# A four-layer pre-norm network on one core: seven of eight groups' first norm and top-8 routing moved from the projection block into the first expert stage

## The reference, cut to what matters

```python
x = x + _L0_attn_ref(_layernorm(x), ...)      # state-space scan, ends in a projection with Wout
x = x + _L0_ffn_ref(_layernorm(x), ...)       # top-8 of 64 experts plus a shared one
x = x + _L1_attn_ref(_layernorm(x), ...)
...
# _L0_ffn_ref
affinity = sigmoid(einsum('bsh,he->bse', hidden_states, router_w))
top_scores, top_idx = top_k(affinity, 8)
top_w = top_scores / (sum(top_scores) + 1e-09)
routed = sum over e of  router_mask[e] * (silu(x @ gate[e]) * (x @ up[e])) @ down[e]
```

## Time and profile before

| | us |
|---|---|
| median of 3 runs | 1939.16 |
| lowest and highest | 1934.07, 1939.63 |
| the profiled execution | 1942.1 |
| its span, from first to last instruction | 1940.4 |
| projection block, first instruction to the first expert instruction | 325.9 to 399.3 |
| first expert stage, 264 chunks | 399.3 to about 1110 |

### The profile page before, as it was taken

The page is one execution under the profiler, slowest core; times in us unless marked ns, Lnnn a source line. Parts: engine busy times, 40 slices in busy tenths (PEclk is TensorE's granted clock), DMA queues, the critical chain, the costliest instruction groups (busy, mean ns, idle before and its releaser), DMA issues.

```text
span 1940.4 us, 25449 instructions
## 1 busy us (share of the span) xinstructions
PE 1724.4 (89%) x8004; PEld 1318.3 (68%) x8004; DVE 1185.5 (61%) x2758; ACT 979.3 (50%) x1906; POOL 852.3 (44%) x866
## 2 busy tenths in 40 slices
PE   6989998779999899999999888889899888888799
PEld 6979997757767677776767655656665555555565
DVE  5542215767677777767686825444356666677765
ACT  3612001656556656565656667666545444445442
POOL 3841201335555545454545453444457666651100
PEclk9989558789999999999999989898899888889999
DMA  6001001087332323233223452221001101002233
GB/s 85 1 2 24 1 1 33 17 198 180 107 93 91 98 85 98 88 98 93 93 88 118 122 149 66 66 86 42 28 12 33 29 23 23 23 31 74 81 109 93
DMA packets 131183, 134.92 MB, mean 70 GB/s; under 512 B 56614, under 2 KB 75306, under 8 KB 131050
## 3 DMA queue, kind: packets, MB, share of 16 engines
q1 hardware_dynamic: 120904, 132.35, 24.5%
q10 hardware_dynamic: 10146, 0.94, 0.6%
HBM read 127.93 MB, written 5.31 MB: 69 GB/s over the span
## 4 chain that ended last, share of the span: by engine, by line
PE 39%; DVE 18%; ACT 12%; issue 7%; POOL 4%; DMA 2%; SPq 1%; DVEq 0%; ACTq 0%; POOLq 0%
PE ypsum L1156 7%; PE flow_G L100 4%; PE flow_G L102 3%; PE flow_G L101 3%; DVE flow_a L1701 2%; DVE flow_a L1707 2%; PE flow_U L100 2%; DVE flow_phi L1485 2%; PE flow_U L101 2%; PE flow_U L102 2%; POOL flow_alo L1790 2%; ACT flow_ahi L1186 1%; ACT xn_tokens L1218 1%; PE flow_side L100 1%; DVE flow_at_rneg L1673 1%
## 5 line engine op out<-in xcount | busy, mean ns | idle before, releaser
L1790 POOL TENSOR_TENSOR flow_alo<-flow_a,flow_ahi 128x512 fp32r<-128x512 f32 x264 | 341.6, 1294 | 339.8 <-ACT flow_ahi L1186 339.3
L100 PE MATMUL flow_G<-xn_hi,flow_hi 128*128 128x512 f32 x520 | 283.9, 546 | 37.6 <-DVE flow_a L1701 22.4
L1701 DVE TENSOR_TENSOR flow_a<-flow_G,flow_mask 128x512 f32<-128x512 f32 x256 | 175.7, 686 | 160.8 <-ACT flow_G L1360 135.4
L1360 ACT ACTIVATE flow_G<-flow_G 128x512 f32<-128x512 f32 x256 | 149.0, 582 | 141.1 <-PE flow_G L102 140.5
L101 PE MATMUL flow_G<-xn_lo,flow_hi 128*128 128x512 f32 x520 | 212.6, 409 | 0.0
L102 PE MATMUL flow_G<-xn_hi,flow_lo 128*128 128x512 f32 x520 | 212.1, 408 | 0.0
L1707 DVE TENSOR_TENSOR flow_a<-flow_U,flow_a 128x512 f32<-128x512 f32 x296 | 204.7, 691 | 9.9
L1186 ACT ACTIVATE flow_ahi<-flow_a 128x512 fp32r<-128x512 f32 x264 | 165.4, 627 | 86.6 <-DVE flow_a L1707 85.5
L1799 POOL TENSOR_TENSOR flow_b<-flow_b,flow_mask 128x512 f32<-128x512 f32 x96 | 126.8, 1327 | 148.5 <-ACT flow_b L1364 77.7
L1799 POOL TENSOR_TENSOR flow_a<-flow_a,flow_mask 128x512 f32<-128x512 f32 x96 | 127.8, 1342 | 105.8 <-ACT flow_a L1364 54.4
L100 PEld LDWEIGHTS flow_G<-xn_hi,flow_hi 128*128 128x128 f32 x520 | 102.2, 197 | 103.9 <-issue 42.2
(11 more groups left out here) (535 smaller groups left out, 3936.3 us busy)
## 6 DMA issues: line engine op xcount, KB each, us to landing
flow_mask<-mask_rows_top SPq DMA_DIRECT2D x512, 128.0 KB, 3.0
flow_mask<-mask_rows_top SPq DMA_DIRECT2D x64, 256.0 KB, 3.2
flow_mask<-mask_rows_zone SPq DMA_DIRECT2D x64, 256.0 KB, 3.2
flow_mask<-mask_rows_steps SPq DMA_DIRECT2D x32, 256.0 KB, 4.0
x<-in_L_attn_x SPq DMA_DIRECT2D x8, 256.0 KB, 5.9
flow_raw<-in_L_ffn_expert_gate_k SPq DMA_DIRECT2D x16, 128.0 KB, 3.6
flow_raw<-in_L_ffn_expert_up_k SPq DMA_DIRECT2D x16, 128.0 KB, 3.6
flow_raw<-in_L_ffn_expert_down_k SPq DMA_DIRECT2D x16, 128.0 KB, 3.9
```

The source lines that it names most:

```text
L100: pe.matmul(out, w_hi, x_hi, start=start, stop=False)
L1360: act.activation(gate, gate, ACT.Silu).then_inc(ev["r_done"], 1)
L1701: dve.tensor_tensor(out, G[at % 2].psum[:, :], weight, ALU.mult).then_inc(ev["t_done"], 1)
L1790: pool.tensor_tensor(alo[i][:, :], acts[i][:, :], ahi[i][:, :].bitcast(F32), ALU.subtract)\
```

## The change

The projection block keeps the product with `wout` and the addition to `x` for all eight groups, but norm, router and top-8 choice for group 0 only, written out in line. The other seven groups get a new kind of side step, "pro", in the flow block: `stats`, `moments`, `rstd`, `normalize`, `x_turn`, `hi`, `lo`, `affinities`, `choose_0` to `choose`, `weights`, `rows`. Group 1's lie in group 0's chunks, group 2's from chunk 29 to 50, group g's (g from 3) in frame g - 2. `exponents` goes to the front of ACT's part of the projection block (its two parameters are loaded first, under a semaphore of their own), the low parts of the 14 matrices go from POOL to DVE, some mask tables of POOL's behind the first norm, and the slabs and the one remaining weight row lie in SBUF where the split experts come later. So `rows_gone` is dropped: DVE waits for the slabs before the low part of chunk 3, and for group 0's row before that of chunk 20.

```diff
-ROUTE_LINKS = {1: 8, 2: 3, 3: 21}
+ROUTE_LINKS = {0: 5, 1: 8, 2: 3, 3: 21}
+LATER_OVER, ROWS_OVER = 3, 20
...
     def place(self, kind, l, g, off):
+        if kind == "pro":
+            if g == 1:
+                return off - (4 if off < 10 else 16)
+            if g == 2:
+                return self.hosts[0].chunks + (off - 5 if off < 10 else off - 21 if off < 28 else off - 20 if off < 31 else off - 19)
+            return (g - 2) * self.hosts[0].chunks + off
...
+PRO_STEPS = {"pe": ((7, "x_turn"), (26.5, "affinities"), (33.7, "weights")),
+             "act": ((4.7, "normalize"), (8, "hi"), (27.5, "affinities"), (34.7, "weights")),
+             "dve": ((1, "stats"), (1.5, "moments"), (9, "lo"), (28, "choose_0"), (29, "choose_1"), (30, "choose_2"), (31, "choose")),
+             "pool": ((2.5, "rstd"),), "sp": ((35.7, "rows"),)}
...
-        def rows_gone(eng):
-            for g in range(GROUPS):
-                eng.wait_ge(k.mask_out[g], 16)
-            eng.wait_ge(k.later_out, 32)
...
-                    if h.index and c == 0:
-                        pe.wait_ge(ev["lo"], plan.norm["att", h.index, g] + 1)
+                    if c == 0 and (h.index or g):
+                        pe.wait_ge(ev["lo"], plan.norm["att" if h.index else "pro", h.index, g] + 1)
...
                 def split_first(c):
+                    if c == LATER_OVER:
+                        dve.wait_ge(k.later_out, 32)
+                    if c == ROWS_OVER:
+                        dve.wait_ge(k.mask_out[0], 16)
...
+                def choose_top8(g, part):
...
+                    if part == 0:
+                        dve.wait_ge(ev["aff"], n + 1)
+                        for j in range(GT):
+                            last = dve.max(best[:, j, :], aff64[:, j, :])
...
+                    if part == 1:
+                        for j in range(GT):
+                            dve.match_replace(marked64[:, j, :], best[:, j, :], aff64[:, j, :], -1.0)
+                        link.then(dve.tensor_reduce(sums, best[:, :, :], AX_X, ALU.add))
...
+                    if part == 2:
+                        link.then(dve.tensor_scalar(tot[:, :], sums, 1e-9, None, ALU.add))
+                        link.then(dve.reciprocal(winv[:, :], tot[:, :]))
...
+                    link.then(dve.scalar_tensor_tensor(out=marked64[:, :, :], in0=marked64[:, :, :], scalar=-1.0, in1=aff64[:, :, :],
+                                                       op0=ALU.is_equal, op1=ALU.mult))
...
+                    dve.tensor_tensor(w64, marked64[:, :, :], winv[:, :].unsqueeze(2).to_broadcast([P, GT, 64]), ALU.mult)\
+                       .then_inc(ev["parts"], 1)
...
 @@ project, ACT @@
-                turns(body, act, after_2=prep.take_squares, after_4=prep.take_others, after_6=prep.take_products,
-                      after_8=prep.exponents)
+                prep.exponents(act)
+                act.wait_ge(ev["shift"], 1)
+                for j in range(GT):
+                    last = act.activation(k.xn[:, j, :], k.x[:, j, :], ACT.Identity, scale=k.rstd[:, j:j + 1], bias=shift[:, j:j + 1])
...
+                prep.take_squares(act)
+                act.wait_ge(ev["logits"], 1)
+                act.activation(aff[:, :, :], logits[:, 0:GT * E].rearrange("p (j e) -> p j e", j=GT), ACT.Sigmoid)\
+                   .then_inc(ev["aff"], 1)
+                prep.take_others(act)
+                prep.take_products(act)
...
 @@ project, DVE @@
+                prep.temperature(dve)
+                prep.low(dve)
...
 @@ project, SP @@
-                send_masks(k, sp, route)
+                sp.wait_ge(k.masks_done, 1)
+                sp.dma_start(k.mask_rows[route.kind][:, 0:GROUP], k.weights_t[:, :]).then_inc(k.mask_out[0], 16)
                 prep.keep(sp)
```

More of the change, by code:

```diff
@@ L685, in steps @@
                         if l < 3 or name in LAST_STEPS]
+                if not l and g:
+                    out += [(self.place("pro", 0, g, off), name, "pro", 0, g) for off, name in PRO_STEPS[engine]]
                 if l:
@@ L2590, in weights @@
-                def weights(g):
-                    pe.wait_ge(ev["parts"], g + 1)
-                    if g:
-                        pe.wait_ge(k.masks_done, g)
-                    for j in range(GT):
-                        last = pe.transpose(turned[0:E, j * P:(j + 1) * P], w[:, j, :], k.ident[:, :])
-                    last.then_inc(ev["parts_turned"], 1)
-                output(0)
-                def body(p):
-                    p(3, weights)
-                    p(-1, output)
-                    p(1, affinities)
-                    p(0, turn)
@@ L2606, in _ @@
[L2606 removed]
+                for g in range(5):
+                    output(g)
+                pe.wait_ge(ev["xn"], 1)
+                for j in range(GT):
+                    last = pe.transpose(X[:, j * P:(j + 1) * P], k.xn[:, j, :], k.ident[:, :])
+                last.then_inc(ev["xn_turned"], 1)
+                output(5)
+                prep.turn_squares(pe)
+                pe.wait_ge(ev["lo"], 1)
@@ new lines, in _ @@
+                for j in range(GT):
+                    last = mm3(pe, logits[:, j * E:(j + 1) * E], tile(k.xh, j), tile(k.xl, j), rh, rl)
+                last.then_inc(ev["logits"], 1)
+                output(6)
+                prep.turn_others(pe)
+                output(7)
+                prep.multiply(pe)
+                pe.wait_ge(ev["parts"], 1)
+                for j in range(GT):
+                    last = pe.transpose(turned[0:E, j * P:(j + 1) * P], w[:, j, :], k.ident[:, :])
+                last.then_inc(ev["parts_turned"], 1)
@@ new lines, in _ @@
+                dve.memset(k.tick_norm[:, :], 0.0)
+                for j in range(GT):
+                    last = dve.bn_aggr(k.moments[:, j, :], k.stats[:, j, :])
+                last.then_inc(ev["moments"], 1)
+                for g in range(1, 5):
+                    add(g)
+                prep.fill(dve)
+                view = lo_hi(k, 0)
+                dve.wait_ge(ev["hi"], 1)
+                dve.tensor_tensor(view(k.xl), X[:, :].rearrange("p (b s) -> p b s", b=GB),
+                                  view(k.xh).bitcast(F32), ALU.subtract).then_inc(ev["lo"], 1)
@@ new lines, in _ @@
+                add(5)
+                dve.wait_ge(ev["aff"], 1)
+                dve.memset(k.tick[:, :], 0.0)
+                for j in range(GT):
+                    last = dve.max(best[:, j, :], aff[:, j, :])
+                link.then(last)
+                dve.memset(k.tick[:, :], 0.0)
+                for j in range(GT):
+                    dve.match_replace(marked[:, j, :], best[:, j, :], aff[:, j, :], -1.0)
+                link.then(dve.tensor_reduce(tot[:, :], best[:, :, :], AX_X, ALU.add))
```

232 lines of the change are left out of this document (100 added, 132 removed).

## The result

The change is faster: median 1916.15 us (4 runs, 1910.07 to 1918.30) against 1939.39 (4 runs, 1934.07 to 1943.29). The profiled execution took 1910.07 us, with a span of 1908.3.

A forecast was written before the change was run, and what follows sets the result against it. The projection block was taken as a latency chain, the first expert stage as nearly full on PE; 32.0 - 5.5 - 0.5 - 18.0 = 8.0 us faster, profiled 1934.1, median 1931, range 1920 to 1944.

The forecast's parts named there:

- the sum: Whole kernel: 32.0 us gained at the first product, less 5.5, 0.5 and 18.0, gives 8.0 us faster.
- Projection block: From the block's start to the flow block's first mask: 361.8 against 394.6, so 32.8 us earlier.
- slow products of PE: Projection block: products 5, 6 and 7 may run slow, each adding up to 1.7 us; 359.4 if all fast.
- late bound: Projection block: the flow block starts at 364.0 if all three chain products of PE are slow.
- Start of the stage: First expert stage, up to its first product: 9.9 us through statistics, shift, normalizing and first Silu, against 9.1 before.
- Frame 0: Stage's first frame: group 1's route costs 5.5 us (3 to 8), plus 0.5 (0 to 3) for SP's order.
- slow small instruction: Frame 0, DVE: up to 1.2 us allowed for one that took 1167 ns in this stage, 0.2 in projection.
- Groups 2 to 7: Later frames of the stage: moved norm and route cost 3.0 us for each of six groups, 18.0 (3 to 43).
- The nearest row is PE's 2.5: Groups 2 to 7: PE's transposes and router, 2.5 us per group, plus ACT's copy, give 3.0.
- all of it hides: Rival, groups 2 to 7: route and norm hide in waits, 1.0 us per group, 20 faster, 1919; chance 0.10.
- The tables come through: Rival, groups 2 to 7: ACT's tables reach the chain, 5.4 us per group, 6.4 slower, 1946; chance 0.14.
- as before: Sign, end of the stage: the last two frames stay at 91.5 us.

The follow-up runs named there:

- rows_gone: As a run: the change with the old wait put back, so ACT begins the stage only after group 0's weight row and both slabs land; 1921.8 us, ratio 0.9899.
- expo_last: The change with the exponents back at the end of ACT's part of the projection block and the temperature on DVE; 1917.7 us, ratio 0.9884.
- low_pool: The change with the projection block's 14 low parts back on POOL, ahead of its last tables; 1918.3 us, ratio 0.9882.
- no_route: The change without the top-8 routes of groups 1 to 7, all using group 0's weight rows, norms kept in the stage; 1903.9 us, ratio 0.9819.
- late_norm1: The change with group 1's normalize, transposes, high and low part placed two chunks later; 1916.6 us, ratio 0.9878.
- keep_late: The change with SP sending the two slabs at the start of the stage instead of the projection block's end; 1915.4 us, ratio 0.9879.
- two_masks: The change with groups 0 and 1 normalized and routed in the projection block, first two masks loaded there, slabs sent by POOL; 1907.5 us, ratio 0.9829.
- route_early: The change with routes of groups 4 to 7 moved right behind the norm in the same frame, with their own table space; 1922.2 us, ratio 0.9920.
- no_table: The change with the moved routes' Sigmoid replaced by Abs, which needs no change of ACT's table; 1911.1 us, ratio 0.9847.

## Why the prediction was wrong

The mechanism was right: a block of latencies was worth more than PE's time. What failed are sizes in the sum. The profiles differ by 32.1 us where the sum has 8.0. Of the 24.1 between, 8.7 are the projection block, 0.2 the start, 7.2 the groups 2 to 7, 2.9 frame 0, all mis-sized to the change's disadvantage, and 5.1 are the part behind the stage, which is chance as far as the traces tell: in the second profile of the change block and start together are 9.0 off, the groups 6.2, frame 0 2.1, and the last part 0.3 the other way.

**Projection block, 32.8 forecast, 41.5 measured.** The flow block's first mask comes at 353.1 where I took 361.8. The steps, in the block's timeline of the change:

```profile
332.12 0.20 ACT L524 ACTIVATE prep_e<-prep_raw_log_temp 128x1 f32<-128x1 f32 x1 [10.61 <-issue]
...
334.38 0.20 ACT L531 ACTIVATE prep_e<-prep_e 128x1 f32<-128x1 f32 x1
334.49 1.63 ACT L2659 ACTIVATE xn_tokens<-x,proj_shift,ln_rstd 128x128 f32<-128x128 f32 x4
...
342.55 0.38 ACT L2665 ACTIVATE proj_affinity<-proj_logits 128x256 f32<-128x256 f32 x1
...
349.22 0.29 ACT L519 ACTIVATE prep_later_consts<-prep_old_r_full 128x128 fp32r<-128x128 f32 x1
```

```profile
325.14 2.69 PE L2628 MATMUL turn<-ssm_wout,ssm_turned 128*128 128x128 f32 x16 [3.81 <-PEq L1974]
327.62 2.96 PE L2628 MATMUL ypsum<-ssm_wout,ssm_turned 128*128 128x128 f32 x16
330.41 1.95 PE L2628 MATMUL turn<-ssm_wout,ssm_turned 128*128 128x128 f32 x16
```

```profile
345.49 0.42 DVE L2713 TENSOR_TENSOR proj_weights<-proj_selected,proj_selected_inverse 128x256 f32<-128x256 f32 x1
...
350.56 0.28 DVE L580 TENSOR_TENSOR prep_later_consts<-prep_old_r_full,prep_later_consts 128x128 fp32r<-128x128 f32 x1
```

- The block began 0.8 sooner, at 325.1; the scan before it varies by that from run to run (324.3 to 326.5 in the runs above).
- The exponents took 2.46, not 3.7: at the front the trace has one load of a table among them, at the end there had been two. Normalizing ended at 336.1, 2.1 ahead of my 338.2.
- I had put 2.4 into the sum for slow products of PE. (Three slow ones at 1.67 make 5.0, so the late bound was 364.4 and not my 364.0; it changes nothing.) From the third product on all six take 1.95 to 2.05 us, here and in the 12 other profiles with a short block, against 1.95 and 3.62 in the earlier trace rows. PE hardly waits between them and has the full clock, as the windows below show: the sigmoid was done at 342.9, not 346.7. The mean clock of 0.70 was that of the old, idle block; I used it for the new, dense one.
- The low parts on DVE were spaced by 0.20, not 0.28, and lay almost wholly beside ACT's high parts: 350.8, not 356.5. From their end to the first mask it took 2.3, not 2.9.

In the prediction's own steps the 8.7 are 2.4 up to the normalized rows, 1.4 from there to the sigmoid, 0.6 to ACT's last high part, 1.3 to the last low part, 0.6 to the first mask, and the 2.4 for slow products.

Windows of before, a fast product, the stretch ahead of a slow one (PE busy for 4.09 of 5.50) and the slow one, then six products of the change (the third number from the end is the granted clock; 0.50 and 1.00 are the two levels, 1.2 and 2.4 GHz):

```profile
360.48:362.43 1.95, 1.95 (x21) 1.95 (x19) 1.54 (x12) 1.95 (x13) 1.60 (x4) 1.00 0.00 0
362.50:368.00 5.50, 4.09 (x26) 3.87 (x26) 4.74 (x27) 3.42 (x9) 1.40 (x3) 0.72 0.10 24
367.99:371.61 3.62, 3.62 (x19) 3.62 (x18) 2.26 (x15) 2.13 (x5) 0.20 (x2) 0.50 0.16 38
```

```profile
330.41:345.45 15.04, 14.80 (x132) 14.25 (x131) 6.83 (x28) 10.93 (x39) 3.40 (x9) 1.00 0.27 56
```

What three parts of the change are worth was tested one by one: expo_last (4.2 at the start), low_pool (2.0 of its 4.6), rows_gone (4.7). That the clock carries the 2.4 is read from the traces; no run varied it alone. The last of the three confirms what I had taken from the earlier trace rows, the 4.7 us of `rows_gone`.

**Start of the stage, 9.9 forecast, 9.7 measured**, by the way described: POOL's shift, ACT's normalizing, the table, Silu.

**Frame 0, 5.5 + 0.5 forecast, 3.1 (second profile 3.9) measured.** A route costs 4.1 there, of which 1.1 to 1.9 is tables. Group 1's norm does not lengthen the frame (no_route's frame 0 is 1.0 shorter than before's): its normalizing stands before the first product. The slow small instruction that I allowed for came, in another place: the choice's last multiplication took 1.49 us beside a subtraction of POOL's, against 0.42 to 0.43 in the six later groups. The two overlap:

```profile
398.53 1.29 POOL L1855 TENSOR_TENSOR flow_alo<-flow_a,flow_ahi 128x512 fp32r<-128x512 f32 x1 [0.92 <-ACT flow_ahi L1207]
398.62 1.49 DVE L1603 TENSOR_TENSOR xn_tokens<-flow_marked,flow_inverse_weight 128x256 f32<-128x256 f32 x1
```

All ten profiles that route group 1 in frame 0 have it, at 1.47 to 1.49; how much of the 1.06 reaches the frame no run shows. late_norm1, keep_late and two_masks show that what comes off the start comes back in frame 0 by half or in full. The reverse does not hold: rows_gone, low_pool and expo_last begin 4.2 to 4.7 later, and their frame 0 is that of the change within 0.5.

**Groups 2 to 7, 18.0 forecast, 10.8 (second profile 11.8) measured**, 1.8 a group instead of 3.0. Here a step of the argument failed and not only a size. "The nearest row is PE's 2.5" took PE's own time of router and transposes for norm and route together; no_route shows 0.8 to 1.6 for a route and 0.1 to 0.6 for a norm in frames 2 to 5, 1.5 for both in the mean. I had argued myself that the router's product, the choice and the tables are covered where DVE is late with the features, and then added PE's 2.5 none the less. The rival *all of it hides*, at 1.0 per group, came nearer to the price of the later frames; frame 1 (4.1 for two groups) kept the mean above it. Its 1919 is near the measured time by luck in part, for it had the block and frame 0 from the same wrong sum. A share of a busy engine, 94%, was my argument against it, and it is no argument: PE waits for 5.9 us in frame 2, and its busy time rose by 2.25 there while the frame grew by 1.4. That the steps are cheap by their place, and not cheap anywhere, is what route_early shows.

**The tables.** *The tables come through* was wrong for frames 2 to 6 and right for groups 1 and 2. The load's own time is 1.28 with no gap ahead (sigmoid at 601.38 for 0.39, load at 601.79), and two of them were worth 2.0 in frame 1 and 1.1 in frame 0 by no_table. By the rule of the Trainium skill, "ScalarE: Activation LUTs", section "What ACT_TABLE_LOAD costs", a drain of 1.38 would come on top of each, 5.3 us for the two as an estimate. The trace does not agree: the load starts 0.02 after the sigmoid's end, the next instruction 0.01 after the load's, and frame 1 gave back 2.0.

**Other signs.** Frame 6 grew too, by 0.9, where I had said "as before": group 7's weights are turned at its beginning. Later stages are as long as before within the scatter (827.0 and 832.3 against 832.0).

## What to carry to other kernels

Price moved work by what the chain does at its new place, chunk by chunk, not by the busy share of the fullest engine: the same route cost 0.8 to 1.6 us under attention's features, 3.3 to 3.4 eighteen chunks earlier (route_early less no_route in frames 3 to 5; frame 2's 5.4 still holds the end of group 3's late route), and 4.1 in frame 0 with less to hide under. Such a place has a size (here the 1.6 us at chunk 29), and one addition more comes through nearly in full. When a block of waits is made dense, its matmuls are to be priced at the clock of a dense block, and the hand-over behind it (issues, landings, the first instructions of every engine) is to be walked through as its own chain.

## What was not expected of the hardware

The time of one program moved by 5.3 us in stages that no edit touched, 3.9 of it in one stretch of 60 us with a granted clock of 0.94 or 0.87. That is as much as expo_last's 4.2 us, which the medians do not show. In all ten profiles with group 1's route in frame 0 one DVE multiplication took 1.47 to 1.49 us beside a POOL subtraction, where it takes 0.42 to 0.43 elsewhere. Eight sends of the weight row (64x512) one behind the other from SP took 4.98 us and held back the end of the block by 4.8, where one took 0.48.
